# The sums of gathered expert rows move half a group of heads later

## The reference, cut to what matters

```
xn   = layernorm(x)
attn = softmax(where(|q - k| > 128, -1e9, q k^T / 4)) v   per head, then w_proj
ffn  = shared(xn) + sum over the 8 chosen experts e of weight_e * down_e(silu(gate_e xn) * up_e xn)
out  = x + attn + ffn
```

## Time and profile before

| | us |
|---|---|
| median of 3 runs (1376.28 to 1380.51) | 1376.39 |
| span of the profiled execution | 1166.2 |
| span of attention in it | 739.8 to 1127.9 |
| one group in the middle of attention | 23.86 |
| busy in such a group: TensorE, VectorE, ScalarE, GpSimd | 22.13, 21.94, 15.58, 15.93 |

### The profile page before, as it was taken

The page is one execution under the profiler, slowest core; times in us unless marked ns, Lnnn a source line. Parts: engine busy times, 40 slices in busy tenths (PEclk is TensorE's granted clock), DMA queues, the critical chain, the costliest instruction groups (busy, mean ns, idle before and its releaser), DMA issues. The chain is left out here.

```text
span 1166.2 us, 33945 instructions
## 1 busy us (share of the span) xinstructions
PE 1085.4 (93%) x8297; PEld 799.0 (69%) x8298; DVE 767.9 (66%) x2491; ACT 756.1 (65%) x1914; POOL 622.2 (53%) x658
## 2 busy tenths in 40 slices
PE   6989799599999999999999999699999999999999
PEld 3545456399999999999999999355545545455457
DVE  7777779734444444444444457589999998999933
ACT  2555367567777777777777776366666666666653
POOL 0444200176666666666666655466666666666620
PEclk9999899899999999999999999799999999999999
DMA  6888811278888888878877764366665576656413
GB/s 223 216 213 213 240 42 32 94 222 261 247 251 244 252 253 240 250 240 250 253 229 205 206 198 149 101 154 159 154 171 142 142 169 161 152 143 159 122 60 122
DMA packets 143000, 213.84 MB, mean 183 GB/s; under 512 B 19425, under 2 KB 115682, under 8 KB 142946
## 3 DMA queue, kind: packets, MB, share of 16 engines
q0 software_dynamic: 27648, 86.02, 27.6%
q1 hardware_dynamic: 70946, 84.42, 25.9%
q10 hardware_dynamic: 44352, 42.74, 10.6%
HBM read 142.59 MB, written 70.26 MB: 183 GB/s over the span
## 5 line engine op out<-in xcount | busy, mean ns | idle before, releaser
L1076 POOL DMA_INDIRECT xb<-token_rows,idx_ring_x x320 | 303.1, 947 | 179.2 <-issue 140.5
L1104 PE MATMUL psum<-xTe,wb_and_xT_all_or_onorm 128*128 128x128 f32 x2560 | 339.2, 276 | 0.0
L1724 POOL DMA_INDIRECT yg<-expert_rows,idx_ring x256 | 254.2, 993 | 122.5 <-PE psum L1452 45.3
L1227 DVE TENSOR_SCALAR ys<-psum,xb 128x256 f32<-128x256 f32 x320 | 154.9, 484 | 244.7 <-PE psum L1113 243.3
L1104 PEld LDWEIGHTS psum<-xTe,wb_and_xT_all_or_onorm 128*128 128x128 f32 x2560 | 312.4, 192 | 0.1
L1566 ACT ACTIVATE pT<-psum 128x384 f32<-128x384 f32 (+1 forms) x512 | 215.5, 467 | 135.6 <-PE psum L1452 127.7
L1626 DVE CUSTOM_DVE_ANT_0 masked<-psum,mask_q 128x384 f32<-128x384 f32 (+1 forms) x480 | 230.9, 518 | 20.6 <-PE psum L1459 17.2
L1177 ACT COPY wb_and_xT_all_or_onorm<-wb_and_xT_all_or_onorm 128x512 f32 x320 | 197.7, 619 | 18.5 <-SPq L1038 4.8
L1113 PE MATMUL psum<-wb_and_xT_all_or_onorm,aT 128*128 x640 | 191.8, 381 | 0.4 <-issue 0.2
L1163 ACT COPY xTe<-psum 128x256 f32<-128x256 f32 x320 | 119.1, 372 | 102.4 <-PE psum L1094 93.0
L1459 PE MATMUL psum<-qk 96*128 96x384 bf16 (+1 forms) x480 | 154.0, 321 | 29.7 <-DVE nmax L1626 18.4
(11 more groups left out here) (143 smaller groups left out, 1143.0 us busy)
## 6 DMA issues: line engine op xcount, KB each, us to landing
expert_rows<-ys ACTq DMA_DIRECT2D x160, 256.0 KB
wb_and_xT_all_or_onorm<-in_w_exp SPq DMA_DIRECT2D x64, 384.0 KB, 4.2
qk<-q_stacks SPq DMA_DIRECT2D x32, 384.0 KB
q_stacks<-wb_and_xT_all_or_onorm SPq DMA_DIRECT2D x32, 192.0 KB, 2.7
qk<-k_parts SPq DMA_DIRECT2D x32, 192.0 KB
k_parts<-wb_and_xT_all_or_onorm SPq DMA_DIRECT2D x28, 192.0 KB, 3.1
token_rows<-rows SPq DMA_DIRECT2D x8, 640.0 KB, 4.3
xb<-token_rows,idx_ring_x POOLq DMA_INDIRECT x320
```

The source lines that it names most:

```text
L1076: nc.gpsimd.indirect_dma_start(out=xb[:, r, :], out_offset=None, in_=rows_d, in_offset=bass.IndirectOffsetOnAxis(ap=idx_ring[:, q, r:r + 1 ...
L1104: last = nc.tensor.matmul(banks[GU + r % NB][:, part * P:(part + 1) * P], wgu[:, r % NW, h, part * I:(part + 1) * I], xT[:, r % NX, h, :], ...
L1227: nc.vector.tensor_scalar(ys[:, r // 2 % YR, r % 2, :], banks[Y + r % 2][:, 0:D], xb[:, r % XR, bass.ds(e + W_COL, 1)], None, ALU.mult).th ...
L1724: nc.gpsimd.indirect_dma_start(out=yg[:, h, k, :], out_offset=None, in_=y_d, in_offset=bass.IndirectOffsetOnAxis(ap=idx_ring[:, h, k:k + 1 ...
```

## The change

The table `SUMS` is turned: the five instructions behind slots 4 to 11 of group g are now those of tile 2g - 1 (h = 1 of the group before), and those behind slots 20 to 27 are those of tile 2g (h = 0). The last tile is summed behind the last group. The gathers' count of key scores is moved with them by 16 slots: those of half h of group g are now spread over slots 16h to 16h + 12 of that same group, where before they were spread over the half group ahead of it. The gathers of the first and of the last group are no longer spread. `copy_slots` on ScalarE and its place are as before.

```
-    SUMS = {(1, 0): (0, 0), (1, 2): (0, 1), (2, 0): (0, 2), (2, 1): (0, 3), (2, 3): (0, 4),
-            (5, 0): (1, 0), (5, 2): (1, 1), (6, 0): (1, 2), (6, 1): (1, 3), (6, 3): (1, 4)}
+    SUMS = {(1, 0): (1, 0), (1, 2): (1, 1), (2, 0): (1, 2), (2, 1): (1, 3), (2, 3): (1, 4),
+            (5, 0): (0, 0), (5, 2): (0, 1), (6, 0): (0, 2), (6, 1): (0, 3), (6, 3): (0, 4)}
...
                         if (j, hh) in SUMS:
-                            combine(g, *SUMS[j, hh])
+                            h, part = SUMS[j, hh]
+                            if h == 0:
+                                combine(g, 0, part)
+                            elif not is_first(g):
+                                combine(g - 1, 1, part)
...
             one_by_one(dve, group)
+            for part in range(NSUM):
+                combine(NG - 1, 1, part)
...
-                    scores = (h - 1) * K * PACE + k * PACE - EARLY
-                    if k >= EARLY and not (is_first(i) and h == 0):
+                    scores = h * K * PACE + k * PACE - EARLY
+                    if k >= EARLY and paced:
...
-            gather(0, 0)
-            gather(0, 1)
-            with pool.Fori(1, NTILE // 2) as i:
+            for h in range(2):
+                gather(0, h, False)
+            with pool.Fori(1, NTILE // 2 - 1) as i:
                 for h in range(2):
-                    gather(i, h)
+                    gather(i, h, True)
+            for h in range(2):
+                gather(NTILE // 2 - 1, h, False)
```

More of the change, by code:

```diff
@@ L1388, in key_back @@
         return {0: 2, 1: 2, 2: 5}.get(j * HG + hh, 3)
-    SUMS = {(1, 0): (0, 0), (1, 2): (0, 1), (2, 0): (0, 2), (2, 1): (0, 3), (2, 3): (0, 4),
-            (5, 0): (1, 0), (5, 2): (1, 1), (6, 0): (1, 2), (6, 1): (1, 3), (6, 3): (1, 4)}
+    SUMS = {(1, 0): (1, 0), (1, 2): (1, 1), (2, 0): (1, 2), (2, 1): (1, 3), (2, 3): (1, 4),
+            (5, 0): (0, 0), (5, 2): (0, 1), (6, 0): (0, 2), (6, 1): (0, 3), (6, 3): (0, 4)}
+    NSUM = 5
     def one_by_one(engine, group):
@@ L1711, in _, with gather @@
             PACE, EARLY = HG * TT // (2 * K), 2
-            def gather(i, h):
+            def gather(i, h, paced):
                 if not is_first(i):
```

## The result

The changed kernel took 1425.05 us (median of 6 runs, 1422.62 to 1430.76) where the kernel before took 1378.72 (6 runs, 1376.28 to 1380.51): a ratio of 1.0337, interval [1.0314, 1.0359], 46.3 us slower. The forecast was 1405.5 with a range of 1387 to 1432.

A forecast was written before the change was run, and what follows sets the result against it. TensorE and VectorE were taken to share the bound. Opening and loop together gave +23.7 us by slot 31 of group 14, the end +3.0 and +2.4: 29.1 on 1376.4, so 1405.5 us, range 1387 to 1432.

The forecast's parts named there:

- The loop: Groups 1 to 14: ScalarE's copy waits for the gather just released, stalling TensorE; +2.09 us for each of 13 groups, 27.2.
- the price of one group, 2.1 us: Loop, groups 2 to 14: a group takes 25.95 us in place of 23.86.
- +1.65 and +0.44: Loop, per group: what the stalls behind slots 27 and 11 add, 1.65 us and 0.44 us.
- clock falls in the stalls: Loop rival: TensorE drops to 1.2 GHz after each stall; 34 us more, 1439, with both halves 1473; chance 0.08.
- 2.4 GHz were granted during the opening stall: Group 0: TensorE's clock stayed full during its 4.86 us stall, then ran at 1.2 GHz for some 5 us.
- The landing, 2.8 us: Loop and end: time from a gather's start until its data can be used, taken as 2.8 us.
- From the scores to the last gather, 1.25 us: Loop, slots 11 and 27: scores counted after 0.44 us, GpSimd answers 0.81 us later.
- the series does not hold gather 7 up any longer: Loop, second half: GpSimd's series starts before slot 31, so gather 7 could start 9.0 us after that slot.
- The opening, -6.6 us: Group 0: moving tile 0's additions removes VectorE's and TensorE's waits; slot 15's key scores start 6.6 us sooner.
- The end, +5.4 us: After group 14: late gathers and last sums add 3.0 us, half clock in the merge 2.4.
- the 210.2 us around its span stay: Whole time: the 210.2 us between the profile's 1166.2 us span and the 1376.4 us median remain unchanged.
- the bounds: Whole time: up to 15 us less if small waits absorb stalls, 22 more for slower waits; 1390 to 1428.

The follow-up runs named there:

- e1: Changed kernel with ScalarE's copies of row numbers moved half a group later; 1391.36 us, ratio 1.0078 to the kernel before.
- e2: Kernel before with ScalarE's second copy of row numbers moved up from behind slot 27 to behind slot 11; 1397.63 us, ratio 1.0105 to the kernel before.
- c0: Kernel before, unchanged, profiled a second time, on a slower chip; 1385.06 us, one execution.
- e7: Changed kernel with each gather in the loop released four key scores earlier, on a quicker chip; 1216.63 us, ratio 1.0415 to the kernel before.
- e8: Kernel before with later sums, and copies moved likewise, in groups 0 and 1 alone, on a slower chip; 1385.67 us, ratio 1.0118.
- run 13: Not a label of any run: the words belong to "loop code that has run 13 times before", said of group 14 in c0.
- e6: Kernel before with the last group's 8 gathers of its second tile not waiting for key scores, on a quicker chip; 1168.42 us, ratio 1.0.
- e9: Kernel before with group 1 as straight code on ScalarE and VectorE, and the last 8 gathers not waiting for scores; quicker chip, 1168.10 us, ratio 1.0001.

## Why the prediction was right, and where it was not

**The loop: mechanism right, the clock left out.** Copy, landing, exponential, TensorE: e1 and e2 show this chain from both sides. The prediction put 30.3 us on groups 1 to 14 (27.2, and 3.1 of the opening's gain given back in group 1); the three profiles of the changed kernel average 457.2 us against c0's 421.7, +35.5. The term mis-sized is the price of one group, 2.1 us against 2.5. By halves, in groups 2 to 14, slot 15 to slot 31 took 16.8 us against c0's 14.9 and slot 31 to slot 15 took 15.8 against 15.2: +1.9 and +0.5, where +1.65 and +0.44 were put. The prediction took only time to wait into account. The rival "clock falls in the stalls" was given 0.08 because nothing tested an idle of 2 us from full clock; the changed trace tests it, and the clock falls at nearly every stall, 25 times. The trace it read held a hint. The prediction says that 2.4 GHz were granted during the opening stall; the clock stood at 0.76 on average from 751 to 753 us and at 0.50 from there, and TensorE only went on at 753.82. So it fell in the stall itself. The Trainium skill ("TensorE: Matmul & The Clock Gate", "HAM oscillation — how this bites in real kernels") says that a kernel which waits for a DMA in each iteration can fall back each time: this trace agrees, with 0.57 and 0.58 granted behind the stall of group 4. But the rival did not add its 34 us on top: the loop has 59 us more at 1.2 GHz than c0's, yet TensorE is busy for only 22.9 us more, and idle for 15.2 more where waiting alone was put at 30.3. Slower matmuls seem to have filled gaps that TensorE had anyway; in c0 it idles 6.2 us a group, and 1.7 in the rows of the prediction. No run held the clock up in the stalls, so how the two share the 35.5 us is not shown. That a sum without the clock came within 5.2 us of the loop is therefore in part luck.

**The landing, 2.8 us: nearly right** (2.95 on average). **From the scores to the last gather, 1.25 us: right behind slot 27 (1.3), too small behind slot 11** (2.3), because the series of gathers is late there. The prediction said that the series does not hold gather 7 up any longer; in this half it does, as e7 showed too. The price of the stall is there not only the last gather's, it is the series'.

**The opening, -6.6 us: right on the kind of chip whose trace was read (-6.2 in e7, and -6.6 up to slot 15), absent on those that were timed (between -0.4 and +1.2).** VectorE's wait of 6.9 us for the landing in group 0 has gone, as predicted; a longer one has come. VectorE and ScalarE in group 0 of the changed kernel:

```profile
870.34 0.56 DVE L1627 CUSTOM_DVE_ANT_0 masked<-psum,mask_q 128x384 f32<-128x384 f32 x1 [11.78 <-remote]
```

```profile
867.41 0.49 ACT L1567 ACTIVATE pT<-psum 128x384 f32<-128x384 f32 x1 [9.44 <-remote]
```

"Remote" means that no instruction of this core released them by the profile. In c0 the same group has such pauses too (10.81 us of ScalarE) beside the landing's 6.92, and lasts as long.

**The end, +5.4 us: +6.7 on a quicker chip (e7), by the predicted mechanism; +9.9 to +12.6 on the slower ones, by another.** In e7 VectorE's last work ends 27.7 us after slot 31 of group 14 in place of 22.7, so +5.0 where +3.0 was put, since the last gather leaves 20.8 us after that slot and not 18.5. On the slower chips the last sums do not stand alone behind attention: the merge begins after 1.07 us of idle time as before, at full clock. It is group 15's key scores that last 31.6 to 34.3 us in place of 21.7, with two common pauses. VectorE, TensorE, and the last gather on GpSimd:

```profile
1359.16 0.21 DVE L1646 COPY nmaxT<-psum 24x128 bf16<-24x128 bf16 x1 [8.76 <-remote]
...
1374.61 0.26 DVE L1653 RECIPROCAL rec<-psum 128x16 f32<-128x16 f32 x1 [8.66 <-remote]
```

```profile
1359.81 0.50 PE L1468 MATMUL psum<-qk 98*128 98x384 bf16 x1 [2.37 <-ACT pT L1567]
1375.26 0.50 PE L1468 MATMUL psum<-qk 98*128 98x384 bf16 x1 [6.06 <-ACT pT L1567]
```

```profile
1371.89 0.95 POOL L1730 DMA_INDIRECT yg<-expert_rows,idx_ring  x1 [0.30 <-issue]
```

Each of these two ends about 2.7 us after the last of eight gathers in a row has started, and each lies in code that the engines run once. The two of e1's end do too (2.0 and 2.8 us), but not every pause fits. ScalarE's of 10.81 us in group 0 of c0 ends with three gathers of the series still to come, the one in group 1 of e8 ends 0.1 us before the last gather starts, and c0 has one of 5.60 us, ended by "remote" at 1301.30, in group 14, which is loop code that has run 13 times before. Neither series nor code was tested alone on a slower chip: e6 and e9, made for it, ran on quicker ones. The cause is open.

**The sum.** 29.1 us were forecast and 46.3 measured. By stages, with the average of the three changed traces against c0, the forecast was off thus: opening 6.8 us too hopeful (40.5 against 40.3), loop 5.2 too small, end 6.0 too small. Two of the three gaps belong to pauses that the trace read does not contain. The step at fault is the one that let "the 210.2 us around its span stay": a span 15% below the time beside it was a sign that trace and time were not of the same condition, and the bounds, made from its rows alone, could not hold what only the other condition does. So it is in part luck that 1425.05 still lies inside 1387 to 1432: of the three terms only the loop's came by the mechanism that was put into the sum.

## What to carry to other kernels

When the release of a transfer is moved, look for every wait on its landing that is not moved with it: here a copy of 0.2 us in ScalarE's queue turned from covered to exposed and cost about 1.3 us each of 28 times. Count a paced series as a whole (release of the buffer, eight issues, landing) against the distance to its consumer; e7 shows that an earlier pace does not help where this sum fills it. And compare the span of a profile with the time it is meant to explain before a single term is priced.

## What the runs showed of the hardware

The kernel before took 1168 us on two chips and 1370 to 1381 on two others, with granted clocks of 0.984 beside e6 and 0.967 in c0. Its merge runs at the same pace on both, but a loop group takes 30.1 us in place of 23.86 and the experts' stage ends at 857.4 in place of 740.4; these are the stages in which GpSimd issues gathers, but no run shows that the gathers are the reason. TensorE's idle time of 1.9 us in two parts, from full clock, was followed by 4 us at mostly 1.2 GHz. In none of the traces did two gathers start less than 1.24 us apart. In the changed trace the data of a gather of 128 rows were usable 2.8 to 3.1 us after it began; in half of e7's waits it took 3.3 to 5.1 us.
